# Order of the beats in an involution and mixture-of-experts kernel: strips first, then the next quad's kernel products

## The chip, the cores and the metric

One core of a Trainium2 chip runs the whole program. The metric is the time of one execution on the device in microseconds (us); lower is better. TensorE multiplies matrices and writes PSUM, VectorE and ScalarE work element by element, GpSimd issues the indirect DMAs and some small powers, SyncE ("SP") issues most other DMAs. Each engine runs its own instructions in order and meets the others at semaphores.

## The reference, cut to what matters

x is (4, 56, 56, 128) in float32. The first half is an involution: every pixel's 7x7 kernel is made from its own features, one for each of 16 groups of 8 channels. The second half sends each of the 12,544 pixels (tokens) through two of eight experts.

```python
xn = layernorm(x)                                           # over channels
r = relu(batchnorm(einsum('bhwc,cd->bhwd', xn, w_reduce)))  # 128 -> 32 channels
kgen = (einsum('bhwd,de->bhwe', r, w_span) + b_span).reshape(B, H, W, 16, 49)
patches = 49 shifted copies of xn, zero padded
x = x + einsum('bhwgk,bhwkgc->bhwgc', kgen, patches)

t = layernorm(x)
probs = softmax(t @ gate_w + gate_b); top2_vals, top2_idx = top_k(probs, 2)
for e in range(8):                                          # cw: the two weights of a token
    out = out + cw[:, e] * (gelu(t @ W1[e] + b1[e]) @ W2[e] + b2[e])
x = x + out
```

## The kernel before, in words

The image is cut into seven **chunks** of eight rows. A chunk has four **quads** (Q0 to Q3 here; the program counts them through, Q = 0 to 27); a quad is one set of four groups (32 channels) over the chunk's eight rows. A quad has four **strips** of two rows. All engines walk the same list of **beats**, 16 to a quad and 64 to a chunk, in which every engine's share of each task has its beat; the order within an engine is thus written out by hand, and semaphores do the rest.

- *Kernel products* (`kernels`, L1148): a quad's 7x7 kernels for 112 pixels at a time. Eight **pairs** of products to a quad; a pair is two times four matmuls and fills both banks of the PSUM tile kg. ScalarE's `take_kernels` (L662) copies a pair from kg to the SBUF buffer kb. A pair's first product waits for the copy of the pair before it (`kb_act`). The pairs of quad Q + 1 are made while quad Q is at work.
- *Strip* (`apply`, L1182): 28 matmuls, each shown as two in the profile, of kb's kernels with a window of padded input rows, into one PSUM bank e. VectorE masks it into conv (`take_conv`, L825), which frees e for the next strip; TensorE turns conv back into pixels (`turn_back`, L1194), and VectorE adds that to the rows (L836).
- *Expert visit* (`expert_visit`, L1243, L1252, L1262): one tile of 128 tokens of an earlier chunk: the first product of tile i, the second product of tile i - 1, and at every second visit the transposes of two further tiles. ScalarE applies the gelu (L712) and copies transposes (L704), VectorE adds the bias (L985) and copies the next tile's weights from a table in SBUF (L976). 36 visits to a chunk, the first 104 beats after its first strip: quads 0 to 5 have none, quad 6 only in its second half. After quad 27 visits are all that TensorE has left.
- *Token traffic*: per chunk GpSimd issues 32 indirect DMAs that scatter normalized tokens to their experts' rows (L569, beats 10 to 32 of the next chunk's time) and 32 that gather the results (L583, beats 43 to 62 of the chunk after that); VectorE mixes what was gathered into the rows (L997). SP stores normalized rows (`put_xn`, L365), loads windows (L382), and moves the experts' rows (L415, L423).
- *Side work* at fixed beats of a chunk: transposes of normalized rows at 11, 20, 29, 38 (L1128) and the channel reduction three beats later (L1133); `apply2` (L677), transposes (L1207) and gates (L1215) of the chunk's tokens from beat 55 on; softmax, ranks and places of the tokens in beats 1 to 10 of the next chunk.

A quad's order on TensorE, with kernels for the next quad in brackets: visit, strip 0 | [pair 0], visit | turn-back, strip 1, visit | [pair 1] | turn-back, strip 2, visit | [pair 2] | turn-back, strip 3, visit | [pair 3] | turn-back, visit | [pair 4] | visit | [pair 5] | visit | [pair 6] | visit | [pair 7].

kb holds six groups, so that two of the next quad's four groups can be written while the strips still read this quad's. Which slots a quad has goes round with Q modulo 3; for Q % 3 == 1 they are not adjacent.

Of the kernel before, what the change touches and what calls it, by code (L numbers as in the profile page):

```python
# [14 lines left out]
def metaformer_kernel(nc, x, w_reduce, gamma, beta, mean, var, w_span, b_span,  # L15
# [20 lines left out]
    UNITS = H // 4  # L36
    KR = 3 * CR + 2
    IMG = 57 + WIN
    GSLOTS = 6
    POS = 16  # L40
    WSLOTS = 5
    HALF = B * PW * 64
# [6 lines left out]
    SLOTS = NT + 1  # L49
    BEATS = 16 * QUADS  # L50
    START = 40
    VISITS = (0, 1, 2, 4, 6, 8, 10, 12, 14)
    PAIRS = (NT + 1) // 2
    SCATTER = (10, 32)
    GATHER = (43, 62)
# [32 lines left out]
    with ctx:  # L88
# [13 lines left out]
        ident = sb("ident", [128, 128])  # L102
        before = sb("before", [T, T])
        ones = sb("ones", [T, T])
        group_mask = sb("group_mask", [128, 6])
        minus_half = sb("minus_half", [128, 8])
        wred3 = sb("wred3", [128, 3 * CR])
        bn_in = sb("bn_in", [3 * CR, 4])
# [504 lines left out]
        def _(act):  # L613
# [41 lines left out]
            def take_kernels(Q, p):  # L655

                g = 4 * Q + p // 2
                act.wait_ge(kg_done, 16 * Q + 2 * p + 2)
                if g >= GSLOTS:
                    act.wait_ge(main_done, 4 * ((g - GSLOTS) // 4 + 1))  # L660
                lo = ((g % GSLOTS) * POS + 8 * (p % 2)) * PATCHES
                act.activation(kb[:, lo:lo + 8 * PATCHES].rearrange("p (h k) -> p h k", h=2),  # L662
                               kg[0:WIN, :].rearrange("p (h k) -> p h k", h=2)[:, :, 0:4 * PATCHES], ACT.Copy) \
                    .then_inc(kb_act, 1)
# [76 lines left out]
            for beat in range(BEATS * (NC + 2)):  # L741
                n, o = divmod(beat, BEATS)
                Q, j = divmod(beat, 16)
                live = n < NC
                if live and Q + 1 < QUADS * NC and j % 2:
                    take_kernels(Q + 1, j // 2)
                if beat == BEATS + START - 1:
                    take_pair(0, 0)
                if visit(beat):
                    expert_visit(*visit(beat))  # L750
                if live:
                    for k in range(4):
                        if o == TURN[k] and 2 * n + 2 + k // 2 < UNITS:
                            take_xnT(2 * (2 * n + 2) + k)
                        if o == REDUCE[k] and 2 * n + 2 + k // 2 < UNITS:
                            features(2 * (2 * n + 2) + k)
                    if o in (1, 3, 5, 7) and 2 * n + 3 < UNITS:
                        apply1(2 * n + 3, o - 1, o + 1)
                    if o in (37, 39, 41, 43) and 2 * n + 4 < UNITS:
                        apply1(2 * n + 4, o - 37, o - 35)  # L760
                    if o in (57, 59):
                        take_tnT(n, (o - 57) // 2)
                    if o in (55, 56):
                        apply2(n, o - 55)
                    if o in (60, 61):
                        apply2(n, o - 58)
                    if o == 62:
                        take_tnT(n, 2)
                if 0 <= n - 1 < NC:
                    if o == 0:  # L770
                        take_tnT(n - 1, 3)
                    if o == 2:
                        exps(n - 1)
# [3 lines left out]
        def _(dve):  # L777
# [40 lines left out]
            def take_conv(t):  # L818

                Q = t // STRIPS  # L820
                turn = 2 if Q % 3 == 1 else 0
                dve.wait_ge(main_done, t + 1)
                if t >= 2:
                    dve.wait_ge(back_done, t - 1)
                nc.vector.tensor_tensor(conv[t % 2][:, :].rearrange("p (g k) -> p g k", g=4),  # L825
                                        e_bank[:, 0:4 * T].rearrange("p (g k) -> p g k", g=4),
                                        group_mask[:, turn:turn + 4].unsqueeze(2).to_broadcast([128, 4, T]),
                                        ALU.mult).then_inc(conv_ready, 1)

            def add_back(Q, hf):  # L830
# [200 lines left out]
            for g in range(G):  # L1031
                ins = dve.tensor_copy(image[:, g], raw[:, g])
            ins.then_inc(wk_step, 1)
            dve.tensor_reduce(group_mask[:, 0:4], ident[:, :].rearrange("p (b g c) -> p g b c", b=4, g=4),
                              AX.XY, ALU.add).then_inc(wk_step, 1)
            dve.wait_ge(wk_step, 3)
            dve.tensor_copy(group_mask[:, 4:6], group_mask[:, 0:2])
            dve.memset(lo_rows[CR:2 * CR, :], 1.0).then_inc(wk_step, 1)
            dve.wait_ge(wk_step, 4)
            for g in range(G):  # L1040
# [67 lines left out]
        def _(pe):  # L1108
# [55 lines left out]
            def apply(t, pw):  # L1164
# [2 lines left out]
                Q, s = divmod(t, STRIPS)  # L1167
                q = Q % QUADS
                w = win[window_no(n, q // 2, s) % WSLOTS]
                first = (4 * Q) % GSLOTS  # L1170
                for b in range(B):
                    p = (s // 2) * 56 + b * 14 + (s % 2) * 7 + pw
                    if Q % 3 == 1:
                        rhs = kb[:, :].rearrange("p (o g i k) -> p o g i k", o=3, g=2, i=POS)[:, 0:3:2, :, :, p]
                        rhs = rhs.rearrange("p o g i -> p o (g i)")
                    else:
                        rhs = kb[:, first * POS * PATCHES:(first + 4) * POS * PATCHES]
                        rhs = rhs.rearrange("p (i k) -> p i k", k=PATCHES)[:, :, p]
                    to = e_bank[32 * b:32 * b + 32, 0:4 * T]
                    to = to.rearrange("p (g a w c) -> p g a w c", g=4, a=2, c=8)[:, :, :, pw, :]  # L1180
                    at = (b * PW + pw) * 64 + (q % 2) * 32
# [111 lines left out]
            for beat in range(BEATS * (NC + 2)):  # L1293
# [6 lines left out]
                if live:  # L1300
                    if j in (2, 4, 6, 8):
                        turn_back(4 * Q + j // 2 - 1)
                    if j < 8 and j % 2 == 0:
                        apply_wait(4 * Q + j // 2)
                        for pw in range(PW):
                            apply(4 * Q + j // 2, pw)
                    if more and j % 2:
                        kernels(Q + 1, j - 1)
                        kernels(Q + 1, j)
                if beat == BEATS + START - 1:  # L1310
                    turn_pair(0, 0, SLOTS - 1)
                if j and visit(beat):
# [51 lines left out]
```

## Time and profile before

| | |
|---|---|
| time, median of 3 runs | 1448.48 us (1446.62 to 1455.89) |
| profiled execution, its own time | 1449.3 us |
| span of its instructions | 1447.5 us |
| busy: PE, PE weight load, DVE, ACT, POOL | 960.6, 838.2, 497.3, 553.9, 488.6 us |
| granted TensorE clock, mean | 0.754 |
| DMA | 144.04 MB, mean 100 GB/s |

In the profile PE is TensorE, PEld its weight loads, DVE VectorE, ACT ScalarE, POOL GpSimd. "L1182" is a line of the kernel. A group such as e<-kb,win names what is written and what is read. The clock is given as a share of full speed (1.00 is 2.4 GHz, 0.50 is 1.2 GHz). The ends of matmuls are modelled: a group's length holds the depth of the array, so the distance from start to start says more. An idle time in brackets stands just before a group, with what ended it; "issue" is one that nothing in the profile explains.

### The profile page before, as it was taken

The page shows a single profiled execution, that of the slowest core. Times are in us where ns is not written, and L with a number is a line of the kernel's source. Part 1 is how long each engine was busy: PE and PEld are TensorE (multiplying, and loading weights), DVE is VectorE, ACT ScalarE, POOL GpSimd, SP SyncE. Part 2 cuts the span into 40 slices and gives each one's busy share as a digit, 9 for nine tenths or more (in the row PEclk, how much of TensorE's full clock was granted, in tenths as well). Part 3 has the DMA queues.
Part 4 walks back from the last instruction along what each step waited for, and adds up shares of the span by engine and source line. Part 5 has one row for each costly group of instructions (what it writes and reads, how often), then busy time and mean ns, then how long its engine had stood idle before and what let it go on. Part 6 is the DMA issues. An engine that isn't in the chain of part 4 may idle for free.

```text
span 1447.5 us, 29676 instructions
## 1 busy us (share of the span) xinstructions
PE 960.6 (66%) x11249; PEld 838.2 (58%) x11249; DVE 497.3 (34%) x1612; ACT 553.9 (38%) x1198; POOL 488.6 (34%) x536
## 2 busy tenths in 40 slices
PE   2687764888197792877928878379694687726540
PEld 1576653687096680876817768268583576725440
DVE  6111230345043450344513444123442235413432
ACT  5244330666054460453614545135351333312220
POOL 3000144012604517035171351712516136254425
PEclk9586665899598785897868778679876787656785
DMA  5659613463154532545425363252631422212322
GB/s 135 138 111 270 134 46 75 90 156 79 48 144 104 117 98 68 123 105 127 99 73 128 88 143 93 75 120 59 138 91 53 100 63 68 76 49 77 96 62 63
DMA packets 184078, 144.04 MB, mean 100 GB/s; under 512 B 65110, under 2 KB 169558, under 8 KB 183488
## 3 DMA queue, kind: packets, MB, share of 16 engines
q1 hardware_dynamic: 168114, 115.03, 33.2%
q0 software_dynamic: 14336, 25.72, 6.7%
q8 instruction: 91, 1.49, 0.4%
q10 hardware_dynamic: 1486, 1.38, 0.4%
q14 instruction: 51, 0.42, 0.1%
HBM read 89.70 MB, written 52.36 MB: 98 GB/s over the span
## 4 chain that ended last, share of the span: by engine, by line
PE 39%; issue 21%; another core or an unknown queue 10%; SPq 7%; ACT 7%; DVE 7%; POOL 3%; DVEq 2%; DMA 1%; ACTq 1%; POOLq 0%
PE e L1182 11%; PE kg L1148 9%; PE hy L1252 5%; PE hy L1262 5%; SPq L365 3%; POOL got L583 2%; PE back L1194 2%; ACT kb L662 2%; PE misc L1215 2%; DVEq L975 2%; ACT tn L677 2%; PE hy L1243 2%; SPq L431 1%; PE misc L1207 1%
## 5 line engine op out<-in xcount | busy, mean ns | idle before, releaser
L662 ACT ACTIVATE kb<-kg 112x896 f32<-112x896 f32 x224 | 205.6, 918 | 451.4 <-PE kg L1148 363.7
L1182 PE MATMUL e<-kb,win 112*32 112x64 f32 x6272 | 241.8, 291 | 182.3 <-issue 165.2
L583 POOL DMA_INDIRECT got<-yrows,pos x224 | 215.9, 964 | 331.9 <-DMA yrows<-yo 141.0
L1148 PE MATMUL kg<-rT,wk 98*112 98x112 f32 x1792 | 270.9, 313 | 75.5 <-ACT kb L662 42.2
L1182 PEld LDWEIGHTS e<-kb,win 112*32 112x32 f32 x6272 | 185.4, 131 | 230.1 <-issue 209.5
L569 POOL DMA_INDIRECT xrows<-tn,pos x224 | 213.8, 954 | 285.0 <-DVE pos L955 151.9
L1148 PEld LDWEIGHTS kg<-rT,wk 98*112 98x112 f32 x1792 | 233.9, 206 | 102.6 <-ACT kb L662 54.3
L712 ACT ACTIVATE hT<-hy,staged 128x128 f32<-128x128 f32 x490 | 152.6, 364 | 287.1 <-PE hy L1252 181.6
L1262 PE MATMUL hy<-staged,hT 128*128 128x128 f32 x980 | 179.7, 313 | 51.1 <-issue 22.3
L825 DVE TENSOR_TENSOR conv<-e,group_mask 128x448 f32<-128x448 f32 x112 | 69.7, 622 | 387.2 <-PE e L1182 258.4
L1252 PE MATMUL hy<-xT,staged 128*128 128x128 f32 x980 | 186.5, 321 | 19.1 <-issue 11.9
L1262 PEld LDWEIGHTS hy<-staged,hT 128*128 128x128 f32 x980 | 155.2, 225 | 57.6 <-issue 30.6
L976 DVE COPY staged<-table 128x642 f32 x245 | 123.5, 504 | 189.2 <-DVE yo L985 146.7
L1252 PEld LDWEIGHTS hy<-xT,staged 128*128 128x128 f32 x980 | 157.7, 228 | 32.7 <-issue 22.5
L985 DVE TENSOR_TENSOR yo<-hy,staged 128x128 f32<-128x128 f32 x245 | 70.5, 288 | 236.4 <-PE hy L1262 143.6
L547 POOL TENSOR_TENSOR rs<-ve,minus_half 112x8 f32<-112x8 f32 x14 | 23.2, 1657 | 275.1 <-DVE ve L796 275.0
L997 DVE SCALAR_TENSOR_TENSOR t_row<-got,wt,t_row 112x128 f32<-112x128 f32 x224 | 73.6, 348 | 51.4 <-DMA got<-yrows,pos 39.3
L1194 PE MATMUL back<-ident,conv 128*112 128x128 f32 x448 | 77.0, 299 | 20.3 <-DVE conv L825 20.3
L1243 PE MATMUL hy<-ident,xin 128*128 128x128 f32 x245 | 59.1, 326 | 18.4 <-DVE yo L985 8.7
L1194 PEld LDWEIGHTS back<-ident,conv 128*112 128x112 f32 x448 | 54.0, 148 | 25.6 <-DVE conv L825 22.9
L704 ACT ACTIVATE xT<-hy 128x256 f32<-128x256 f32 x126 | 47.9, 380 | 11.4 <-PE hy L1243 11.4
L1243 PEld LDWEIGHTS hy<-ident,xin 128*128 128x128 f32 x245 | 30.9, 162 | 28.1 <-issue 14.7
(113 smaller groups left out, 602.3 us busy)
## 6 DMA issues: line engine op xcount, KB each, us to landing
win<-xpad SPq DMA_DIRECT2D x56, 784.0 KB
xin<-xrows SPq DMA_DIRECT2D x56, 256.0 KB
yrows<-yo SPq DMA_DIRECT2D x56, 256.0 KB
t_row<-in_x_dram SPq DMA_DIRECT2D x64, 112.0 KB
xpad<-xs SPq DMA_DIRECT2D x240, 28.0 KB
out_dram<-t_row SPq DMA_DIRECT2D x56, 112.0 KB
xs<-in_x_dram SPq DMA_DIRECT2D x48, 112.0 KB
xrows<-tn SPq DMA_DIRECT2D x4, 896.0 KB, 14.6
```

The costliest lines, as they stand in the source:

```text
L569: pool.indirect_dma_start(xrows[n % 2], bass.IndirectOffsetOnAxis(ap=pos[n % 2][:, i:i + 1], axis=0), tn[:, c * C:(c + 1) * C], None) \
L583: pool.indirect_dma_start(got[:, slot * C:(slot + 1) * C], None, yrows[n % 2], bass.IndirectOffsetOnAxis(ap=pos[n % 2][:, k * COLS + c:k * ...
L662: act.activation(kb[:, lo:lo + 8 * PATCHES].rearrange("p (h k) -> p h k", h=2), kg[0:WIN, :].rearrange("p (h k) -> p h k", h=2)[:, :, 0:4 ...
L712: ins = act.activation(hT_at(n, i)[:, f * 128:(f + 1) * 128], h_at(i)[:, f * 128:(f + 1) * 128], ACT.Gelu, bias=staged_at(n, i)[:, 2 * HID ...
L976: dve.tensor_copy(staged_at(n, i)[:, :], table[:, bass.ds(at, ROW)]).then_inc(weights_in, 1)
L997: dve.scalar_tensor_tensor(out=to, in0=got[:, (i % 8) * C:(i % 8 + 1) * C], scalar=wt[n % 2][:, k * COLS + c:k * COLS + c + 1], in1=to, op ...
L1148: mm = pe.matmul(kg_bank[j % 2][0:WIN, i * PATCHES:(i + 1) * PATCHES], wk[:, at:at + WIN], r[:, :, :, b4 + i], start=True, stop=True, skip ...
L1182: mm = pe.matmul(to, w[:, at:at + 32], rhs, start=True, stop=True, skip_group_check=True)
L1194: mm = pe.matmul(back[0:T, s * 128:(s + 1) * 128], conv[t % 2][:, x_ * T:(x_ + 1) * T], ident[:, :], is_transpose=True, start=(x_ == 0), s ...
L1243: mm = pe.transpose(turned_at(i)[:, h * 128:(h + 1) * 128], xin[k % 2][:, at:at + C], ident[:, :])
L1252: mm = pe.matmul(h_at(i)[:, f * 128:(f + 1) * 128], staged_at(n, i)[:, f * 128:(f + 1) * 128], xT_at(i // 2)[:, at:at + 128], start=True, ...
L1262: mm = pe.matmul(y_at(i), hT_at(n, i)[:, f * 128:(f + 1) * 128], staged_at(n, i)[:, HID + f * C:HID + (f + 1) * C], start=(f == 0), stop=( ...
```

## The change

The buffer kb shrinks from six groups to four, and the beats are dealt out anew. The pairs of the next quad move from the odd beats to beats 8 to 15, one to a beat, on TensorE and on ScalarE. Their eviction now waits until all four strips of the quad before have read kb. The visits move to beats 0, 1, 3, 5, 7, 9, 11, 13 and 15. With four groups every quad's kernels lie in the same order, so the special pattern and the turned mask go. The new order on TensorE: visit, strip 0 | visit | turn-back, strip 1 | visit | turn-back, strip 2 | visit | turn-back, strip 3 | visit | turn-back, [pair 0] | [pair 1], visit | [pair 2] | [pair 3], visit | [pair 4] | [pair 5], visit | [pair 6] | [pair 7], visit. Beats of all other work, and the number of every instruction but one small copy, stay as they are.

```diff
--- before.py
+++ after.py
@@ -36,7 +36,7 @@
     UNITS = H // 4
     KR = 3 * CR + 2
     IMG = 57 + WIN
-    GSLOTS = 6
+    GSLOTS = 4
     POS = 16
     WSLOTS = 5
     HALF = B * PW * 64
@@ -49,7 +49,7 @@
     SLOTS = NT + 1
     BEATS = 16 * QUADS
     START = 40
-    VISITS = (0, 1, 2, 4, 6, 8, 10, 12, 14)
+    VISITS = (0, 1, 3, 5, 7, 9, 11, 13, 15)
     PAIRS = (NT + 1) // 2
     SCATTER = (10, 32)
     GATHER = (43, 62)
@@ -102,7 +102,7 @@
         ident = sb("ident", [128, 128])
         before = sb("before", [T, T])
         ones = sb("ones", [T, T])
-        group_mask = sb("group_mask", [128, 6])
+        group_mask = sb("group_mask", [128, 4])
         minus_half = sb("minus_half", [128, 8])
         wred3 = sb("wred3", [128, 3 * CR])
         bn_in = sb("bn_in", [3 * CR, 4])
@@ -656,8 +656,8 @@
 
                 g = 4 * Q + p // 2
                 act.wait_ge(kg_done, 16 * Q + 2 * p + 2)
-                if g >= GSLOTS:
-                    act.wait_ge(main_done, 4 * ((g - GSLOTS) // 4 + 1))
+                if Q:
+                    act.wait_ge(main_done, STRIPS * Q)
                 lo = ((g % GSLOTS) * POS + 8 * (p % 2)) * PATCHES
                 act.activation(kb[:, lo:lo + 8 * PATCHES].rearrange("p (h k) -> p h k", h=2),
                                kg[0:WIN, :].rearrange("p (h k) -> p h k", h=2)[:, :, 0:4 * PATCHES], ACT.Copy) \
@@ -742,8 +742,8 @@
                 n, o = divmod(beat, BEATS)
                 Q, j = divmod(beat, 16)
                 live = n < NC
-                if live and Q + 1 < QUADS * NC and j % 2:
-                    take_kernels(Q + 1, j // 2)
+                if live and Q + 1 < QUADS * NC and j >= 8:
+                    take_kernels(Q + 1, j - 8)
                 if beat == BEATS + START - 1:
                     take_pair(0, 0)
                 if visit(beat):
@@ -818,13 +818,12 @@
             def take_conv(t):
 
                 Q = t // STRIPS
-                turn = 2 if Q % 3 == 1 else 0
                 dve.wait_ge(main_done, t + 1)
                 if t >= 2:
                     dve.wait_ge(back_done, t - 1)
                 nc.vector.tensor_tensor(conv[t % 2][:, :].rearrange("p (g k) -> p g k", g=4),
                                         e_bank[:, 0:4 * T].rearrange("p (g k) -> p g k", g=4),
-                                        group_mask[:, turn:turn + 4].unsqueeze(2).to_broadcast([128, 4, T]),
+                                        group_mask[:, :].unsqueeze(2).to_broadcast([128, 4, T]),
                                         ALU.mult).then_inc(conv_ready, 1)
 
             def add_back(Q, hf):
@@ -1031,10 +1030,9 @@
             for g in range(G):
                 ins = dve.tensor_copy(image[:, g], raw[:, g])
             ins.then_inc(wk_step, 1)
-            dve.tensor_reduce(group_mask[:, 0:4], ident[:, :].rearrange("p (b g c) -> p g b c", b=4, g=4),
+            dve.tensor_reduce(group_mask[:, :], ident[:, :].rearrange("p (b g c) -> p g b c", b=4, g=4),
                               AX.XY, ALU.add).then_inc(wk_step, 1)
             dve.wait_ge(wk_step, 3)
-            dve.tensor_copy(group_mask[:, 4:6], group_mask[:, 0:2])
             dve.memset(lo_rows[CR:2 * CR, :], 1.0).then_inc(wk_step, 1)
             dve.wait_ge(wk_step, 4)
             for g in range(G):
@@ -1167,15 +1165,9 @@
                 Q, s = divmod(t, STRIPS)
                 q = Q % QUADS
                 w = win[window_no(n, q // 2, s) % WSLOTS]
-                first = (4 * Q) % GSLOTS
                 for b in range(B):
                     p = (s // 2) * 56 + b * 14 + (s % 2) * 7 + pw
-                    if Q % 3 == 1:
-                        rhs = kb[:, :].rearrange("p (o g i k) -> p o g i k", o=3, g=2, i=POS)[:, 0:3:2, :, :, p]
-                        rhs = rhs.rearrange("p o g i -> p o (g i)")
-                    else:
-                        rhs = kb[:, first * POS * PATCHES:(first + 4) * POS * PATCHES]
-                        rhs = rhs.rearrange("p (i k) -> p i k", k=PATCHES)[:, :, p]
+                    rhs = kb[:, :].rearrange("p (i k) -> p i k", k=PATCHES)[:, :, p]
                     to = e_bank[32 * b:32 * b + 32, 0:4 * T]
                     to = to.rearrange("p (g a w c) -> p g a w c", g=4, a=2, c=8)[:, :, :, pw, :]
                     at = (b * PW + pw) * 64 + (q % 2) * 32
@@ -1304,9 +1296,9 @@
                         apply_wait(4 * Q + j // 2)
                         for pw in range(PW):
                             apply(4 * Q + j // 2, pw)
-                    if more and j % 2:
-                        kernels(Q + 1, j - 1)
-                        kernels(Q + 1, j)
+                    if more and j >= 8:
+                        kernels(Q + 1, 2 * (j - 8))
+                        kernels(Q + 1, 2 * (j - 8) + 1)
                 if beat == BEATS + START - 1:
                     turn_pair(0, 0, SLOTS - 1)
                 if j and visit(beat):
```

## Rows read from the trace of the kernel before

**Rows 1.** The page, part 4: the chain that ended last, and part 1, TensorE.

```profile
PE 960.6 (66%) x11249; PEld 838.2 (58%) x11249; DVE 497.3 (34%) x1612; ACT 553.9 (38%) x1198; POOL 488.6 (34%) x536
...
PE 39%; issue 21%; another core or an unknown queue 10%; SPq 7%; ACT 7%; DVE 7%; POOL 3%; DVEq 2%; DMA 1%; ACTq 1%; POOLq 0%
```

**Rows 2.** Timeline of TensorE in quad 14: start us, length us, group, [idle before].

```profile
615.18 1.74 PE L1182 MATMUL e<-kb,win 112*32 112x64 f32 x56
616.85 0.71 PE L1252 MATMUL hy<-xT,staged 128*128 128x128 f32 x4
...
617.76 1.02 PE L1148 MATMUL kg<-rT,wk 98*112 98x112 f32 x8
618.61 0.62 PE L1194 MATMUL back<-ident,conv 128*112 128x128 f32 x4
619.15 1.76 PE L1182 MATMUL e<-kb,win 112*32 112x64 f32 x56
```

**Rows 3.** Timeline of TensorE, pairs with visits between them.

```profile
603.96 1.02 PE L1148 MATMUL kg<-rT,wk 98*112 98x112 f32 x8
...
605.98 1.02 PE L1148 MATMUL kg<-rT,wk 98*112 98x112 f32 x8
```

**Rows 4.** Timeline of TensorE in quad 0: two strips, then pairs, without visits.

```profile
70.20 1.75 PE L1182 MATMUL e<-kb,win 112*32 112x64 f32 x56
...
73.27 1.75 PE L1182 MATMUL e<-kb,win 112*32 112x64 f32 x56
...
76.98 1.02 PE L1148 MATMUL kg<-rT,wk 98*112 98x112 f32 x8 [0.56 <-ACT kb L662]
79.01 1.02 PE L1148 MATMUL kg<-rT,wk 98*112 98x112 f32 x8 [1.01 <-ACT kb L662]
```

**Rows 5.** Groups by line: shapes, count | busy us, mean ns | idle before.

```profile
L662 ACT ACTIVATE kb<-kg 112x896 f32<-112x896 f32 x224 | 205.6, 918 | 451.4 <-PE kg L1148 363.7 <-remote 83.3 <-issue 3.4
...
L677 ACT ACTIVATE tn<-t_row,nb,rs 112x128 f32<-112x128 f32 x112 | 45.7, 485 | 1.5 <-POOL nb L560 1.5
```

**Rows 6.** Timeline of TensorE at half clock: the prologue's pairs, a visit.

```profile
52.69 1.74 PE L1148 MATMUL kg<-rT,wk 98*112 98x112 f32 x8 [1.01 <-ACT kb L662]
55.44 1.74 PE L1148 MATMUL kg<-rT,wk 98*112 98x112 f32 x8 [1.01 <-ACT kb L662]
...
684.47 1.09 PE L1252 MATMUL hy<-xT,staged 128*128 128x128 f32 x4
...
686.20 0.97 PE L1215 MATMUL misc<-gate_sb,r_lin 128*112 128x8 f32 x5
```

**Rows 7.** Windows: from:to, length, busy us (count) by engine, clock, DMA share, GB/s.

```profile
38.90:57.00 18.10, 12.00 (x56) 10.96 (x56) 0.00 (x0) 5.50 (x6) 1.68 (x2) 0.50 0.72 156
77.00:86.80 9.80, 7.11 (x38) 5.61 (x38) 0.22 (x1) 6.23 (x9) 0.00 (x0) 0.68 0.41 86
881.20:911.70 30.50, 29.39 (x421) 26.75 (x422) 18.18 (x59) 20.88 (x43) 3.80 (x4) 0.98 0.43 102
357.00:398.00 41.00, 8.11 (x44) 3.77 (x33) 1.29 (x3) 0.90 (x3) 26.89 (x29) 0.54 0.21 59
1011.40:1064.10 52.70, 38.17 (x412) 34.07 (x412) 22.76 (x82) 21.86 (x52) 26.56 (x28) 0.73 0.51 118
```

**Rows 8.** Timeline of TensorE during GpSimd's bursts: scatter, gather, and the tail.

```profile
353.38 1.29 PE L1148 MATMUL kg<-rT,wk 98*112 98x112 f32 x8
...
456.25 1.74 PE L1148 MATMUL kg<-rT,wk 98*112 98x112 f32 x8 [4.94 <-ACT kb L662]
...
1280.27 1.20 PE L1262 MATMUL hy<-staged,hT 128*128 128x128 f32 x4 [7.91 <-issue]
```

**Rows 9.** Masks and turn-backs (timeline, page part 5), and a strip's product (line L1182: ns min/median/max).

```profile
617.00 0.62 DVE L825 TENSOR_TENSOR conv<-e,group_mask 128x448 f32<-128x448 f32 x1 [0.53 <-PE e L1182]
...
L1194 PE MATMUL back<-ident,conv 128*112 128x128 f32 x448 | 77.0, 299 | 20.3 <-DVE conv L825 20.3
...
L1182 PE MATMUL e<-kb,win x6272: 267/289/317, 63.0 to 1209.5; 112*32 112x64 f32 x196
```

## The prediction, made before the changed kernel was run

> **What bounds the kernel now.** I read the page first: TensorE is busy for 66% of the span and holds 39% of the chain that ended last, with a further 21% "issue"; no other engine holds over 10% [rows 1]. So the question is what TensorE's in-order queue meets. The timeline of a dense stretch tells it: a strip lasts 1.7 us, an expert visit 0.91 (616.85 to 617.76), a pair of kernel products 0.85 (617.76 to 618.61), a turn-back 0.54, and each starts where the one before ends [rows 2]. Two kernel pairs with a visit between them, at 603.96 and 605.98, are 2.02 us apart, and neither waits [rows 3]. With nothing between, they are as far apart (76.98 to 79.01), now with 1.01 us of idle time put down to ScalarE's eviction into kb [rows 4]. A pair owns both banks of kg, so the loop is product 0.85, eviction 0.92 [rows 5] and two hand-overs of together 0.26. At half clock it is 2.75 us [rows 6].
>
> The windows show two other costs. One strip of each chunk from 1 on is stretched to some 40 us: from 357 to 398 TensorE has 44 matmuls, while GpSimd issues 29 indirect DMAs [rows 7]. In the tail, where no strip is left, a visit's products also wait 7.91 us for "issue" in such a burst [rows 8]. I read this as TensorE's instructions coming slowly while GpSimd issues, whatever they are. And the quad of a chunk's gathers lasts 52.7 us, against 30.5 for one without a burst [rows 7].
>
> **The change, part by part.** The work is the same; the order on TensorE and ScalarE is new.
>
> (a) *Quads with visits.* Before, four pairs stood between strips and four between visits. Now eight pairs follow in eight beats, with a visit in every second. In four intervals nothing covers the eviction, and each idles 2.03 - 0.85 = 1.18 us (as much at half clock, where all of TensorE's part is longer). 4 x 1.18 = 4.7. Quads 6 to 26 have visits and a next quad's kernels: 21 x 4.7 = **+99 us**.
>
> (b) *Quads without visits* (0 to 5, and the first half of 6). Before, four pairs lay in the wait strip, mask (0.62 on VectorE), turn-back, which passes anyway: strips were 3.07 us apart (70.20 to 73.27) [rows 4, 9]. Now that wait is bare and strips stay as far apart, but all eight pairs stand in the loop: four more at 2.03 to 2.75 us. The stretch of pairs at 77 to 86.8 had a mean clock of 0.68, the longer one of the prologue 0.50 [rows 7], so the four come at half clock: 6 x 4 x 2.75 = 66, and 4 x 0.85 for quad 6: **+69 us** (52 to 70).
>
> (c) *Masks that come late.* The mask after a strip is now covered by one visit (0.91), just enough for one that starts at once (617.00 is 0.08 behind the strip's end; with 0.62 it ends before 617.76); before, a pair more (0.85) stood there [rows 2, 9]. Where VectorE is behind (softmax and ranks in Q0, moments and mixes in Q3), this shows: some four strips in each of six chunks. All such waits sum to 20.3 us before [rows 9]. Bounds 0 and 84 x 0.85 = 71; nearest to the low end, since most strips find VectorE idle: 24 x 0.6 = **+15**.
>
> (d) *ScalarE's other work.* In beats 8 to 15 stand three of the four groups of apply2 (four activations of 0.485 us each [rows 5]) and half of the features; each lengthens a loop that has 1.1 us to spare in every second interval. Bounds 0 and 7 x 5; **+10**.
>
> (e) *Given back.* TensorE's side work in beats 8 to 15 (transposes of xn and tn, channel reduction, gates) can lie in the new gaps. Bounds -32 (7 x 4.6) and 0; **-20**.
>
> (f) *Gaps that don't count.* During bursts instructions come slowly anyway: 41 us pass with 44 matmuls [rows 7], some three pairs and their visits. Two gaps of each scatter burst and half of the gather quad's are hidden: 6 x 2 x 1.18 + 5 x 2 x 1.18 = 26. Besides, a burst bites only some us after its start: a pair at 353.38 ran at its usual speed within the burst that then held the strip [rows 8]. If TensorE first uses up what it was handed before, it does so for longer in a stretch that has gaps already. The first gathers held a pair for 4.94 us [rows 8]; I give back 2.5 for each of 12 bursts. Bounds -90 and -20; **-55**.
>
> (g) *The clock.* With half the gaps filled it may fall or stay. At half clock a visit takes 1.73 us (684.47 to 686.20) [rows 6], so an interval with one is 1.55 + 1.73 instead of 2.03, one without 2.75: 4 x 1.25 + 4 x 0.72 = 7.9 us a quad. Some twelve of the 21 were near full clock. Bounds 0 and 95; the nearer row is that of pairs alone for half of the intervals and the dense quad (0.98) for the others [rows 7]; I take a quarter, **+25**.
>
> (h) At nothing: the even pattern of kb (one product of a strip is 267 to 317 ns over all quads, whichever pattern they read [rows 9]); one small copy less on VectorE; the eviction's wait for the last strip, done before the turn-back that precedes pair 0; windows, each with some 17 us of pairs ahead of its strip (it would cost if SP's stores of xn ran later than that); visit 35, which still follows strip 3 directly, so that the last rows are stored and the gathers start as before. SP, GpSimd and VectorE keep their beats. The visits of beats 15 and 0 now meet, but visit 0's own products cover the gelu between them.
>
> Sum: 99 + 69 + 15 + 10 - 20 - 55 + 25 = +143. Against the profiled execution's own 1449.3 (span 1447.5), 0.8 above the median of 1448.5, that gives **1592 us**. All bounds together would give 1478 and 1799; (c) and (g) at their upper ends would need every mask late and every clock down, so I stop at 30 and 60 of them, with (d) at 20, (e) at -15 and (f) at -40: 1673.
>
> **A rule to weigh.** The stretch of pairs at 77 to 86.8 kept TensorE busy for 7.1 of 9.8 us at a clock of 0.68, a dense quad had 0.98 [rows 7]. The Trainium skill, page "TensorE: Matmul & The Clock Gate", section "HAM oscillation", says that waits between bursts of matmuls put the clock back to half. The trace agrees for pairs alone; no row shows pairs with visits at every second place. By that rule in full (g) would be at its upper end, which is the first rival.
>
> **The rivals.**
> 1. *The clock falls in all second halves*: (g) at 95, 1660 us. For: the rows above. Against: visits fill half of the gaps.
> 2. *The gaps are swallowed*: more quads than I think are bound by VectorE, the gathers or slow instructions, and mainly the quads without visits pay: 69 and a third of 99, less 25 for a fuller (f): 1525 us. For: ScalarE and VectorE chains fill much of Q3's 52.7 us. Against: the dense quads' queue has no idle time to swallow anything.
> 3. *Faster.* Only a strip's instructions suffer under the bursts, as the pair at 353.38 suggests. Now five pairs and three visits (13 us) would lie between a burst's start and the next strip, instead of 4: 9 us saved each, 54 in all, 1540. It becomes faster than before only if pairs and visits hold at least 4 + 143/6 = 28 of a burst's 40 us; with the stretched strip gone altogether (38 x 6) it ends at 1364. Against: the tail's visits are slow too [rows 8].
> 4. *It doesn't do what it says*: pairs overlap their eviction after all, 1450 us. Each pair's first product waits for the eviction before it, so the code speaks against it.
>
> **How the numbers follow.** Chances: forecast 0.62 (its own range 1540 to 1640), clock 0.15, swallowed 0.15, faster 0.05, no effect 0.03. The range 1505 to 1670 leaves out the last two and half of the clock's. A measurement of this kernel tells about 1% from no change: faster 0.05, same 0.03, slower 0.92.
>
> **What would show it.** In the changed profile: kg's products idle for kb by some 1 us at every second pair, over 100 us in all; strips of a quad some 3.2 us apart with one visit between; busy time of ScalarE and VectorE as before; a dense quad of 34 to 37 us instead of 30.5; the 40 us of a burst still there, now begun on pairs. It would be wrong by a dense quad of 31 (2), a granted clock near 0.6 in the second halves (1), or bursts that pairs pass unhindered (3).

## The result, and the profile after

The changed kernel takes 1618.5 us (median of 4 runs, 1618.1 to 1625.9) where the kernel before takes 1452.2 in the same comparison: a ratio of 1.116, with a 95% interval of 1.110 to 1.122. The profiled execution has a span of 1624.2 us at a mean clock of 0.714, against 1447.5 at 0.754.

The page of the changed kernel, parts 1 and 4, answers to [rows 1]:

```profile
PE 1070.4 (66%) x11249; PEld 945.9 (58%) x11249; DVE 494.6 (30%) x1611; ACT 565.3 (35%) x1198; POOL 484.9 (30%) x536
...
PE 45%; another core or an unknown queue 18%; issue 10%; ACT 9%; DVE 7%; POOL 3%; DVEq 3%; SPq 2%; DMA 1%; ACTq 1%; POOLq 0%
PE kg L1146 14%; PE e L1174 9%; PE hy L1244 6%; ACT kb L662 6%; PE hy L1254 6%; PE back L1186 3%; DVEq L974 2%; POOL got L583 2%; PE misc L1207 2%; PE hy L1235 2%; DVE staged L975 1%; PE misc L1199 1%; DVE conv L824 1%; PE misc L1131 1%
```

The number of matmuls is the same and TensorE is busy for 110 us more: its instructions have become slower. VectorE (495 for 497) and ScalarE (565 for 554) do what they did. The kernel products now lead the chain, and part 5 says what they wait for (the kg group, its eviction, the turn-backs; busy us, mean ns | idle before, releaser):

```profile
L1146 PE MATMUL kg<-rT,wk 98*112 98x112 f32 x1792 | 336.3, 353 | 219.7 <-ACT kb L662 176.3
...
L662 ACT ACTIVATE kb<-kg 112x896 f32<-112x896 f32 x224 | 205.2, 916 | 413.4 <-PE kg L1146 238.8
...
L1186 PE MATMUL back<-ident,conv 128*112 128x128 f32 x448 | 77.6, 301 | 33.2 <-DVE conv L824 32.8
```

ScalarE's eviction costs the same as in [rows 5], but the products wait 176 us for it. Before, it was this (waits of TensorE, kernel before: total, times, longest):

```profile
PE kg L1148 <- ACT kb L662: 42.2, 32, 5.1
```

**Where the time came from.** Windows from strip 0 to strip 0 divide the span (columns as in [rows 7]). The kernel before; its prologue is 63.0 us, and the rows are quads 0 to 6, quads 7 to 26, and the last quad with the tail:

```profile
63.00:294.00 231.00, 169.87 (x2274) 143.21 (x2274) 55.22 (x180) 92.52 (x148) 40.48 (x43) 0.71 0.49 117
294.00:1189.80 895.80, 640.29 (x8016) 564.70 (x8017) 325.33 (x1022) 374.92 (x817) 318.71 (x333) 0.80 0.41 100
1189.80:1447.50 257.70, 127.20 (x878) 113.66 (x878) 92.65 (x292) 60.70 (x188) 116.15 (x122) 0.66 0.26 70
```

The same three of the changed kernel, whose prologue is 62.3 us:

```profile
62.30:337.60 275.30, 186.01 (x2276) 155.77 (x2276) 55.46 (x180) 89.67 (x140) 41.36 (x44) 0.69 0.42 100
337.60:1361.60 1024.00, 737.80 (x8014) 666.36 (x8013) 323.47 (x1022) 386.50 (x820) 314.10 (x331) 0.71 0.36 87
1361.60:1624.20 262.60, 122.31 (x879) 106.59 (x878) 91.70 (x293) 60.21 (x186) 116.26 (x122) 0.69 0.26 69
```

So 44 us came in quads 0 to 6, 128 in quads 7 to 26, and 5 in the tail. In the middle part TensorE's clock fell from 0.80 to 0.71 and its busy time rose by 98 us for the same matmuls.

One chunk shows how. Quads 8 to 11 of the kernel before: a dense one, one with the stretched strip, one light, one with the gathers:

```profile
326.30:356.40 30.10, 29.29 (x418) 26.72 (x418) 17.69 (x58) 21.37 (x45) 2.98 (x4) 1.00 0.29 66
356.40:425.30 68.90, 35.83 (x396) 29.26 (x396) 13.80 (x41) 16.32 (x36) 29.20 (x31) 0.68 0.40 100
425.30:460.10 34.80, 28.50 (x388) 25.33 (x388) 14.63 (x43) 19.92 (x44) 9.47 (x11) 0.89 0.33 81
460.10:512.30 52.20, 38.17 (x413) 34.66 (x412) 22.33 (x80) 21.28 (x50) 27.76 (x29) 0.73 0.53 122
```

And of the changed kernel, with the second halves (the eight pairs) of quads 8 and 9 below:

```profile
379.70:455.90 76.20, 40.90 (x418) 36.83 (x416) 18.59 (x60) 22.87 (x48) 30.35 (x32) 0.65 0.26 64
455.90:491.80 35.90, 31.52 (x399) 28.59 (x400) 13.79 (x40) 16.28 (x34) 1.87 (x2) 0.83 0.54 124
491.80:533.90 42.10, 34.52 (x390) 31.00 (x392) 13.31 (x40) 19.66 (x41) 9.50 (x10) 0.71 0.29 73
533.90:590.20 56.30, 43.94 (x417) 39.61 (x416) 22.47 (x82) 22.33 (x51) 26.76 (x28) 0.64 0.46 107
...
394.60:455.98 61.38, 26.84 (x133) 24.39 (x133) 10.16 (x34) 14.42 (x28) 30.35 (x32) 0.57 0.20 54
468.04:491.76 23.72, 19.34 (x128) 17.80 (x129) 7.82 (x27) 13.67 (x26) 1.87 (x2) 0.79 0.49 114
```

The scatter burst moved from quad 9's strip into quad 8's pairs and kept its price: it stretched a strip of 1.7 us to some 41 [rows 7], and it now makes a second half of 23.7 us last 61.4. The quads without a burst of scatters pay besides: 7.3 us in quad 10, 4.1 in quad 11, and the first two together 13.1. No quad in that chunk is at full clock any more; the dense one before was.

The timeline of TensorE in quad 20 of the changed kernel shows both halves (start, length, group, idle before). It answers to [rows 2, 3]:

```profile
1016.98 1.80 PE L1174 MATMUL e<-kb,win 112*32 112x64 f32 x56
...
1020.67 0.65 PE L1186 MATMUL back<-ident,conv 128*112 128x128 f32 x4 [0.62 <-DVE conv L824]
...
1026.28 1.03 PE L1146 MATMUL kg<-rT,wk 98*112 98x112 f32 x8
1028.31 1.02 PE L1146 MATMUL kg<-rT,wk 98*112 98x112 f32 x8 [1.01 <-ACT kb L662]
...
1030.34 1.02 PE L1146 MATMUL kg<-rT,wk 98*112 98x112 f32 x8
1032.37 1.02 PE L1146 MATMUL kg<-rT,wk 98*112 98x112 f32 x8 [1.01 <-ACT kb L662]
```

In this stretch every pair begins 2.03 us after the last. Where a visit lies between, nothing idles; at each second place 1.01 us does. In quads without visits it is every place, and the clock gives way after two such gaps (quad 1 of the changed kernel, answering to [rows 4]):

```profile
109.11 1.03 PE L1146 MATMUL kg<-rT,wk 98*112 98x112 f32 x8
111.39 1.02 PE L1146 MATMUL kg<-rT,wk 98*112 98x112 f32 x8 [1.26 <-ACT kb L662]
113.42 1.74 PE L1146 MATMUL kg<-rT,wk 98*112 98x112 f32 x8 [1.01 <-ACT kb L662]
116.16 1.75 PE L1146 MATMUL kg<-rT,wk 98*112 98x112 f32 x8 [1.01 <-ACT kb L662]
```

### The profile page after: what moved, and what is told of

Same layout as the page of the kernel before. It is cut to its first block, busy times and chain, and to the rows that moved or that the text cites. A ratio compares the mean times of both kernels' runs of the same rounds, so it can differ in the third digit from the quotient of the medians.

```text
span 1624.2 us, 29679 instructions
## 1 busy us (share of the span) xinstructions
PE 1070.4 (66%) x11249; PEld 945.9 (58%) x11249; DVE 494.6 (30%) x1611; ACT 565.3 (35%) x1198; POOL 484.9 (30%) x536
## 4 chain that ended last, share of the span: by engine, by line
PE 45%; another core or an unknown queue 18%; issue 10%; ACT 9%; DVE 7%; POOL 3%; DVEq 3%; SPq 2%; DMA 1%; ACTq 1%; POOLq 0%
PE kg L1146 14%; PE e L1174 9%; PE hy L1244 6%; ACT kb L662 6%; PE hy L1254 6%; PE back L1186 3%; DVEq L974 2%; POOL got L583 2%; PE misc L1207 2%; PE hy L1235 2%; DVE staged L975 1%; PE misc L1199 1%; DVE conv L824 1%; PE misc L1131 1%
## 5 line engine op out<-in xcount | busy, mean ns | idle before, releaser
L1146 PE MATMUL kg<-rT,wk 98*112 98x112 f32 x1792 | 336.3, 353 | 219.7 <-ACT kb L662 176.3
L1146 PEld LDWEIGHTS kg<-rT,wk 98*112 98x112 f32 x1792 | 301.1, 260 | 255.8 <-ACT kb L662 205.9
L1254 PE MATMUL hy<-staged,hT 128*128 128x128 f32 x980 | 203.1, 344 | 119.3 <-ACT hT L712 82.5
L1254 PEld LDWEIGHTS hy<-staged,hT 128*128 128x128 f32 x980 | 177.8, 255 | 125.4 <-ACT hT L712 85.0
L1174 PE MATMUL e<-kb,win 112*32 112x64 f32 x6272 | 212.1, 291 | 44.8 <-issue 21.9
L1244 PE MATMUL hy<-xT,staged 128*128 128x128 f32 x980 | 208.6, 349 | 12.8 <-DVE yo L984 6.9
L1174 PEld LDWEIGHTS e<-kb,win 112*32 112x32 f32 x6272 | 173.1, 130 | 73.9 <-issue 49.2
L1244 PEld LDWEIGHTS hy<-xT,staged 128*128 128x128 f32 x980 | 176.1, 252 | 26.2 <-issue 14.7
L996 DVE SCALAR_TENSOR_TENSOR t_row<-got,wt,t_row 112x128 f32<-112x128 f32 x224 | 74.9, 348 | 42.6 <-DMA got<-yrows,pos 34.8
L1235 PE MATMUL hy<-ident,xin 128*128 128x128 f32 x245 | 64.1, 349 | 23.8 <-DVE yo L984 19.7
L677 ACT ACTIVATE tn<-t_row,nb,rs 112x128 f32<-112x128 f32 x112 | 45.8, 483 | 20.2 <-POOL nb L560 20.2
```

The lines of the kernel that those rows point to most:

```text
L1146: mm = pe.matmul(kg_bank[j % 2][0:WIN, i * PATCHES:(i + 1) * PATCHES], wk[:, at:at + WIN], r[:, :, :, b4 + i], start=True, stop=True, skip ...
L1174: mm = pe.matmul(to, w[:, at:at + 32], rhs, start=True, stop=True, skip_group_check=True)
L1235: mm = pe.transpose(turned_at(i)[:, h * 128:(h + 1) * 128], xin[k % 2][:, at:at + C], ident[:, :])
L1244: mm = pe.matmul(h_at(i)[:, f * 128:(f + 1) * 128], staged_at(n, i)[:, f * 128:(f + 1) * 128], xT_at(i // 2)[:, at:at + 128], start=True, ...
L1254: mm = pe.matmul(y_at(i), hT_at(n, i)[:, f * 128:(f + 1) * 128], staged_at(n, i)[:, HID + f * C:HID + (f + 1) * C], start=(f == 0), stop=( ...
```

## The experiments

My theory was the prediction's: the gaps between pairs, the clock they pull down, and bursts that cost as before. Its rivals: the new place of the visits (ranks, neighbours), the smaller buffer, and gaps that are swallowed or cost nothing in themselves. The ratios are to the kernel before on the same chip, with 95% intervals; that kernel's medians there were 1454 to 1470 us. First four runs, on one chip.

**The visits alone** (kernel before, with the list of visits of the change):

```
-    VISITS = (0, 1, 2, 4, 6, 8, 10, 12, 14)
+    VISITS = (0, 1, 3, 5, 7, 9, 11, 13, 15)
```

> The kernel before with the visits' beats of the change alone (0, 1, 3, 5, 7 and the odd ones up to 15); pairs stay at the odd beats and kb keeps six groups. Theory A (pairs with nothing between them wait for their own eviction, and these gaps also halve the clock): every pair still has a visit or a strip next to it, so the time is that of before, 1440 to 1465 us. Theory B (the visits' new places, the two that meet at beats 15 and 0, and masks covered by a visit alone are what costs): it keeps a good part of the loss, 1490 us or more.

Measured: 1484.7 us, 1.012 (1.007 to 1.017), between the two bands expected. Two small waits grew, the ranks' matmul for VectorE's sums (7.6 us in quads 7 to 26, before 1.3) and a visit that directly follows another (timeline of this kernel, TensorE):

```profile
352.49 0.36 PE L1225 MATMUL misc<-cum,before 112*112 112x8 f32 x2 [1.50 <-DVE cum L918]
...
366.63 0.60 PE L1262 MATMUL hy<-staged,hT 128*128 128x128 f32 x3 [0.61 <-issue]
```

Most of the 17 us lies elsewhere. Quad 7, for one, lasts 38.3 us instead of 32.3 with its clock at 0.82 instead of 0.98 (kernel before, then this one):

```profile
294.00:326.30 32.30, 28.01 (x413) 25.89 (x412) 14.82 (x54) 20.50 (x49) 4.83 (x6) 0.98 0.74 172
296.30:334.60 38.30, 33.80 (x417) 31.40 (x420) 14.54 (x54) 21.01 (x50) 4.36 (x6) 0.82 0.56 131
```

This run does not test the masks, though theory B names them: with the pairs still at the odd beats a mask is covered by a pair and a visit as before, and the turn-backs wait 6.8 us in all for theirs, less than the 20.3 of the kernel before. Moving visits explains some 17 us of the 166, not the rest.

**The order alone**, on the buffer of six groups (the changed kernel with GSLOTS = 6 and the old reading pattern and waits):

```
-    GSLOTS = 4
+    GSLOTS = 6
```

> The whole new order of beats, but on the six-group buffer of before with its turned pattern and its earlier eviction. Theory A: the order is all, so within 1% of the changed kernel, 1605 to 1635 us. Theory C (the four-group buffer costs: the eviction's wait for the last strip, other addresses): clearly below the changed kernel, under 1590.

Measured: 1629.5 us, 1.110 (1.104 to 1.116). The intervals of this kernel and of the changed one overlap. The buffer costs nothing that can be told, and the whole loss is the order, the visits' places included.

**Gaps filled with unread matmuls** (changed kernel; behind each pair with no visit behind it, four products of ident by ident go into the strip's bank, where nobody reads them):

```
+                        if not visit(beat):
+                            for f in range(4):
+                                pe.matmul(e_bank[:, f * 64:f * 64 + 128], ident[:, :], ident[:, :],
+                                          start=True, stop=True, skip_group_check=True)
```

> The changed kernel with four matmuls that nobody reads (identity by identity, 128 columns, into the PSUM bank e, which is idle between the last mask and the next strip) behind every pair that has no visit behind it. They lie in gaps of 1.2 us and add no wait; the output stays as it is. Theory A with the clock as a term of its own (the half clock in the stretches of pairs is a consequence of the gaps, and costs some 60 us of the 170): the granted clock there rises from 0.6 to 0.85 or more, and the time falls by 30 to 70 us, to 1550 to 1590. If the gaps alone cost and the clock doesn't matter: 1618 or a little more, since four matmuls of 0.11 to 0.21 us each just fit into a gap. If the fillers don't fit: up to 1640.

Measured: 1626.3 us, 1.111 (1.104 to 1.118), with the clock at 0.782 instead of 0.714. The clock rose and the time did not fall, so what I expected missed. The second halves of quads 9 and 20 of this kernel show two sides:

```profile
456.68:476.92 20.24, 19.22 (x160) 17.45 (x160) 7.62 (x27) 13.34 (x26) 1.87 (x2) 1.00 0.50 121
1014.30:1080.13 65.83, 31.77 (x164) 29.96 (x164) 10.36 (x34) 14.38 (x28) 30.40 (x32) 0.60 0.22 57
```

and that of quad 20 of the changed kernel:

```profile
1023.04:1078.87 55.83, 20.45 (x134) 17.93 (x133) 9.33 (x32) 13.42 (x25) 30.24 (x32) 0.63 0.27 68
```

Without a burst the half is at full clock and 3.5 us shorter than its 23.72. Quad 20, with a burst, is 10 us longer for its 16 more matmuls (32 as the profile counts them), but it is the extreme. Quad 8 with the same burst is as long as before (changed kernel, then this one):

```profile
379.80:456.00 76.20, 40.90 (x420) 36.81 (x420) 18.50 (x60) 22.77 (x47) 30.35 (x32) 0.65 0.26 64
366.90:443.00 76.10, 36.65 (x449) 32.93 (x448) 18.41 (x60) 22.33 (x46) 30.22 (x32) 0.75 0.26 64
```

In quads 8, 12, 16, 20 and 24 together 388.8 us stand against 372.8, so the fillers cost 3.2 us a quad, or 0.2 us each. In the gathers' quads 11, 15, 19 and 23 it is 232.5 against 223.6. All other quads up to 26 together are 35 us shorter. Fillers pay where no burst is and cost where one is, and the profiled executions end 9 us apart.

**The eviction in two**: one activation for each bank of kg, and each product of a pair waits for its own bank alone, so that products and evictions overlap:

```
+                for h in range(2):
+                    if h:
+                        act.wait_ge(kg_done, 16 * Q + 2 * p + 2)
+                    act.activation(kb[:, lo + 4 * h * PATCHES:lo + 4 * (h + 1) * PATCHES],
+                                   kg_bank[h][0:WIN, 0:4 * PATCHES], ACT.Copy).then_inc(kb_act, 1)
...
-                if j % 2 == 0 and pair:
-                    pe.wait_ge(kb_act, pair)
+                if pair:
+                    pe.wait_ge(kb_act, 2 * pair - 1 + j % 2)
```

> The changed kernel with the eviction cut in two: one activation for each bank of kg, and a product waits only for the eviction of its own bank. The loop of a pair goes from 2.03 to some 1.25 us (a product 0.43, an eviction of 448 columns 0.54, hand-overs 0.26; ScalarE needs 1.08 for two). Theory A: the gap of an uncovered pair falls from 1.18 to 0.4 us: 0.8 x (21 x 4 + 6 x 8) = 105 us, and the clock comes back in part, 20 to 50 more: 1465 to 1515 us. Theory B or C (visits, masks or the buffer cost): at most the 10 to 20 us that the uncovered pairs of quads 0 to 5 save, over 1590.

Measured: 1522.5 us, 1.039 (1.034 to 1.045), a little above the band expected: 0.077 of the 0.116 are gone, 112 us. The timeline of this kernel has two pairs 1.26 us apart where they stood 2.03:

```profile
104.53 1.06 PE L1148 MATMUL kg<-rT,wk 98*112 98x112 f32 x8 [0.88 <-ACT kb L665]
105.79 1.06 PE L1148 MATMUL kg<-rT,wk 98*112 98x112 f32 x8 [0.20 <-ACT kb L665]
```

The next four, on another chip, ask whether the gain is the order's, what the clock is worth away from most bursts, and what the bursts cost either kernel.

**The same split on the kernel before:**

> The kernel before with the eviction cut in two by banks. There pairs with nothing between exist only in quads 0 to 5 (four of them), so Theory A gives 6 x 4 x 0.8 = 20 us less at most, and against it 0.16 us more ScalarE time a pair, which is off the path: ratio 0.985 to 0.995. If evictions were a general bound of this kernel (more than the gaps), it would gain over 3%.

Measured: 1454.4 us, 0.995 (0.991 to 0.999). The split is worth 0.5% there and 7.7% in the changed kernel: it takes away what the new order brought.

**Fillers away from most bursts** (as above, in quads 0 to 3 and in those whose number leaves 1 or 2 when divided by four):

```
+                        if not visit(beat) and (Q < 4 or Q % 4 in (1, 2)):
```

> The fillers of after_fill only in quads 0 to 3 and in the second and third quad of each chunk, away from most of GpSimd's bursts. After_fill raised the clock from 0.71 to 0.78 and shortened the clean second halves (quad 9: 23.7 to 20.2 us, quad 1: 21.9 to 17.7), yet its whole time did not fall; the halves with bursts grew (quad 20: 55.8 to 65.8, quad 11: 35.6 to 38.2). Theory A (the clock costs 3 to 4 us in a clean second half, and every instruction added under a burst costs 0.7 us): 4 x 4 + 12 x 3 = some 40 to 50 us below the changed kernel, ratio to before 1.075 to 1.09. If the half clock costs nothing on balance: the ratio stays at 1.11.

Measured: 1593.4 us, 1.089 (1.083 to 1.096), clock 0.772. The 16 quads give back 0.027, some 39 us (the two intervals leave 26 to 52). The gaps are still there, filled by work that serves nothing, so this part is the clock's. Of the 46 us between the two profiled executions 17 lie in quads 0 to 6 and 29 in quads 7 to 26.

**Scatters spread** (kernel before): the chunk's scatters go over beats 10 to 35 instead of 10 to 32, and GpSimd waits in each beat for TensorE's last strip, pair or visit ahead of it.

```
-    SCATTER = (10, 32)
+    SCATTER = (10, 35)
...
+                    if o > SCATTER[0] and rows_moved(o, SCATTER):
+                        pace(beat)
...
+            def pace(beat):
+                found = gate_of(beat)
+                if found:
+                    pool.wait_ge({"strip": main_done, "pair": kb_act, "visit": gelu_done}[found[0]], found[1])
```

> The kernel before, with GpSimd's 32 scatters of a chunk spread over beats 10 to 35 instead of one burst of 40 us: from the second beat on GpSimd waits, at each beat, until TensorE has reached the strip, pair or visit of the beat before. The work is unchanged. Theory D (while GpSimd issues indirect DMAs TensorE gets an instruction only every 0.7 us; what it was handed before hides the first microseconds of each): short bursts with pauses hide part of the 40 us: 10 to 25 us less in each of seven chunks, ratio 0.89 to 0.95. Rival (the price is one per DMA, 1.25 us each, however they are spaced): within 1% of before. Rival (the stretched strip has another cause, such as SP's stores): within 1% too, with a strip of 36 to 42 us still in the trace.

Measured: 1353.8 us, 0.924 (0.918 to 0.930). The longest strip lasts 12.9 us instead of 41.6, and the kernel is 7.6% faster with the same scatters.

**The same spreading in the changed kernel:**

> The changed kernel with the same pacing. Theory D: as there, 10 to 25 us less in each of seven chunks, 1450 to 1550 us on the scale of the changed kernel's 1618 (ratio 1.00 to 1.07). The difference between the orders should stay near 170 us, if the loss of the change has nothing to do with bursts; if the bursts' falling on pairs is what costs, the difference shrinks to under 100.

Measured: 1470.5 us, 1.003 (1.000 to 1.007). The two orders now differ by 0.080, against 0.116 with bursts: some 117 us, between the two cases expected (near 170, under 100).

The last three, on a third chip, join the two repairs.

**Kernel before, with split eviction and scatters spread** over beats 14 to 37 (a beat with a strip is gated by its strip):

> The kernel before with the eviction cut by banks and with its scatters spread over beats 14 to 37, each beat's scatters waiting for the strip, pair or visit of the beat before (for beat 0 of a quad the strip). Scattering began late in the earlier paced kernel (the places are ready only near beat 13), so its first beats still came as a burst and a strip of 12 us was left. If slow instructions under GpSimd are all of it: ratio 0.90 to 0.925 (0.924 for pacing alone, 0.995 for the cut alone, a little more from the later start). If the later end of the scatters (beat 37, one before SP loads the first rows) holds up the experts: 0.93 or more.

Measured: 1323.8 us, 0.913 (0.906 to 0.920), the lowest median of all. Many of its scatters stand apart, released by TensorE's work or ScalarE's (timeline of GpSimd):

```profile
339.80 1.10 POOL L590 DMA_INDIRECT xrows<-tn,pos  x1 [2.41 <-PE e L1207]
343.08 0.94 POOL L590 DMA_INDIRECT xrows<-tn,pos  x1 [2.19 <-ACT hT L737]
```

In the changed kernel they come back to back:

```profile
420.65 0.94 POOL L569 DMA_INDIRECT xrows<-tn,pos  x1 [0.30 <-issue]
```

The quad that held the stretched strip lasts 42.8 us instead of 68.9 (window of this kernel):

```profile
334.97:377.81 42.84, 35.17 (x394) 31.05 (x394) 14.66 (x42) 17.46 (x44) 21.03 (x22) 0.76 0.62 150
```

Seven of the scatters now fall into the next quad, which lasts 40.6 us instead of 34.8; quads 8 to 11 together take 162.5 instead of 186.0.

**The same with the gathers gated too** (one more line, `pace(beat)` ahead of a beat's gathers):

> The same, with the 32 gathers of a chunk waiting in the same way. The gather quad lasts 52 us against 30 for a dense one and was not helped by pacing the scatters. Theory D: its first burst of eight and the groups of four hold TensorE as the scatters did, so pacing takes 5 to 10 us from each of five chunks: 0.02 to 0.03 lower than the run without. Rival: GpSimd itself is the bound there (32 gathers of 1.25 us and two powers lie in 21 beats), and waiting more only delays the mixes: the same or slower.

Measured: 1329.0 us, 0.915 (0.909 to 0.921): no gain beside 0.913. The gathers' quad is bound by something else; by what is not settled.

**The changed order with both repairs:**

> The changed kernel with both: eviction by banks, scatters paced over beats 14 to 37. Order and everything else as in the changed kernel. Theory A: with the gaps down to 0.4 us and the bursts out of the way what is left of the order's price is 21 x 4 x 0.4 = 34 us, 6 x 4 x 1.25 = 30 for the pairs that no mask wait covers any more, and 15 for late masks and the two visits that meet: 60 to 90 us above the run of the old order with both edits. If the order's price were mostly something else (visits, masks): 120 us or more above it.

Measured: 1371.8 us, 0.943 (0.937 to 0.949). With the gaps at 0.2 to 0.3 us instead of 1.01 and the scatters spread, the new order is still 0.030 behind the old. The medians are 48 us apart, less than the 60 to 90 expected.

## Why the prediction was right, and where its terms were not

The sign, the mechanism and the range held: 1618.5 us lies 26 above the forecast. It is 169 more than the 1449.3 that the forecast started from, where the sum said 143. The terms agree less well than the total. By step:

(a) *Uncovered pairs*: right. 1.01 us idle at each second pair, and the wait for kb went from 42 to 176 us. In quads 7 to 26 it went from 20 to 129: 46 waits under 1.6 us with 48 us together, and 19 longer ones with 81, most of them in quads with bursts or gathers. The wait alone is thus no measure of the term. Splitting the eviction is a better one: it gives back 112 us in this order and 8 in the old. In quads 7 to 26 of the profiled executions it gives back 75 (949.3 for 1024.0), where 80 gaps, each shortened by 0.77, make 62.

(b) *Quads without visits*: too large. Forecast 69, and with quad 6's share 74; measured 44. Quads 0 and 1 paid 9.9 and 9.3, near the 11 of the step, and quad 6 10.2 for 8. Quads 2 to 5 together paid only some 15 instead of 44 (5.6, 0.7, and 8.5 for quads 4 and 5, which hold the first burst). Why so little, no run shows.

(c) *Late masks*: near in all (13 us for 15), wrong in place. The turn-backs wait 33 us for their mask instead of 20. Nearly the whole rise lies in quads 0 to 6 (15 for 4); in quads 7 to 26, where the step had most of its late masks, it is 16 for 15. The ranks' matmul waits 7.6 us there instead of 1.3, but it does so too when only the visits move, so that belongs to (h).

(d), (e) *ScalarE's other work, and side work in the gaps*: ScalarE was busy 11 us more. The trace shows (d) in quad 11: four activations of apply2 (1.65 us at 557.77) stand ahead of an eviction, and the pair behind waits 1.87 us instead of 1.01. No run tells the size of these two terms from (g).

(f) *Gaps that don't count under bursts*: for the scatters this step failed. I gave back 55 us, on the ground that instructions come slowly there anyway and that a burst bites late. For a burst of scatters the price is 61.38 - 23.72 = 37.7 us after, against 41 less a strip's 1.7, 39, before: some 2 us swallowed for each, where the step had about 5. The split says it again: it gives back 50 us in the ten quads 8, 9, 12, 13, 16, 17, 20, 21, 24 and 25, where 40 gaps shortened by 0.77 make 31. In the four gathers' quads (11, 15, 19, 23) it gives back nothing, 223.7 us for 223.6. There the gaps do lie under something, as the step said, though these quads still became 3.6 us longer each. Had the scatter bursts hidden gaps, spreading them would have uncovered these and moved the orders apart; it gives the old order 0.076 and the new 0.113, and they come closer, by 0.036, 53 us. Why they come closer is not shown.

(g) *The clock*: the size is not settled. I took a quarter of its bound, 25 us. The fillers show 39 in 16 quads, but five of these have no visits and their half clock belongs to (b); in quads 7 to 26 of the profiled executions it is 29, with most of the quads under a burst or the gathers not filled. What the clock costs there no run tells. I had put half of the intervals at the dense quad's clock because a visit lies in them. That reading was wrong: the second half came out at 0.79 even without a burst (quad 9), and the light quad 10 went from 0.89 to 0.71. Here the page "TensorE: Matmul & The Clock Gate" of the Trainium skill, section "HAM oscillation", pointed the right way: waits between bursts of matmuls put the clock back. Its own case has waits for DMAs that are longer than the matmuls between them, so it does not by itself speak of waits as short as these. The trace agrees in direction: the waits here are of 1.0 us, and the clock of quads 7 to 26 fell from 0.80 to 0.71.

(h) *At nothing*: the buffer and the pattern, right (the order on six groups). The visits' move at nothing, wrong: by itself it costs 17 us (1.012, 1.007 to 1.017), and only a little of that is the meeting of two visits (0.6 us where it shows) and the ranks' wait.

In quads 7 to 26 (a) to (g) summed to 69 and 128 came, 6.4 for each quad instead of 3.5. The scatters' part of (f) and the visits' move are shown to be in that gap of 59; no run divides the rest. Quads 0 to 6, at 44 instead of 74 and more, hid half of it in the total. Errors of opposite sign made the sum look better than its parts, and that is luck. The lower end of the range, 1505, has no sum behind it. The reading that one strip of each chunk is stretched to some 40 us was also too simple: four of six are (36.0 to 41.6), and in quads 17 and 25 the strip has 23.5 and 12.0 us and what follows it the rest of the burst.

Of the rivals, the clock's (1660) had the right direction and too large a size; swallowed gaps (1525) hold at most for the quads of the gathers. "Faster", by strips alone suffering, is refuted: pairs and visits are held as well. The forecast signs were there. The dense quads 8, 12, 16, 20 and 24 all hold a burst now; the quads without one that follow them last 34.0 to 37.3 us, against the 34 to 37 named. Quad 7, without one too, went from 32.3 to 42.2.

**Still open**: why a burst slows TensorE. That it is the burst of indirect DMAs is shown by spreading them, with only their times and GpSimd's waits changed. It is not the transfers' volume: the DMA engines are 21% busy in it [rows 7]. Whether the supply of TensorE's instructions, its semaphores or the writing of descriptors is what gets in its way was not tried.

## What to carry to other kernels

A loop of product and eviction that owns both banks has a gap somewhat longer than the eviction (1.01 us for 0.92 here); in an in-order queue only the instructions written between two pairs can fill it, so count, for each interval, what covers it, before moving work from one to another. If the cover must go, split the eviction by bank first: it cost nothing here (0.995) and took back two thirds of the loss. And where another engine issues a burst of DMAs, look for the burst itself: the reordering of TensorE's work tried here bought nothing against it, and spacing the same DMAs by TensorE's own progress was worth more than anything else tried.

## What the runs showed of the hardware

While GpSimd issues 32 indirect DMAs back to back, 1.25 us apart, TensorE starts few instructions for the 40 us that they last: the 56 matmuls of one strip (as the profile counts them) took 41.6 us before, 0.74 each, and in quad 8 of the changed kernel 71 matmuls stand in 40 us (408 to 448). Matmuls added to a quad with a burst cost 0.2 us each on average, not 0.74; that would fit if what finds no place in the 40 us runs behind them at its usual pace, but no run shows it. A higher mean clock is no measure of time by itself: the kernel with fillers has the same time at 0.78 as the changed one at 0.71. In quad 1 the granted clock was 0.96 from 109.1 to 113.4 us, over two pairs with gaps of 1.3 and 1.0 us, and 0.50 (1.2 GHz) from there to 129.9, with gaps of 1.0 before most pairs.
